# Attention scores in fp32 on four row tiles instead of bf16 parts, in a kernel of two expert layers and one windowed attention

## What is computed

```python
x = x + 0.5 * ffn(layernorm(x))       # top-1 router, 16 experts, capacity 320 in token order, gelu
x = x + attn(layernorm(x))
x = x + 0.5 * ffn(layernorm(x))

def attn(x):                          # 8 query heads, 4 key heads, head size 16
    q, k, v = rope(x @ Wq), rope(x @ Wk), x @ Wv      # each key head serves 2 query heads
    scores = q @ k.T / 4
    scores += head_scales * (q[..., :3] @ head_dirs) * (k[..., :3] @ head_dirs)
    allowed = (j <= i) & ((j < 4) | (j >= i - 127))   # window of 128 and 4 sinks
    return softmax(where(allowed, scores, -inf)) @ v @ Wo
```

## Time and profile before

| | us |
|---|---|
| median of 3 runs | 583.79 (583.53 to 583.94) |
| span of the profiled execution | 586.0 |
| PE busy | 462.1 (79%) |
| DVE busy | 349.6 (60%) |
| ACT busy | 319.4 (55%) |
| POOL busy | 225.0 (38%) |

### The profile page before, as it was taken

How to read it: one execution, slowest core, us unless ns; L and a number is a source line. 1 busy time by engine, 2 the same in 40 slices (tenths; PEclk the granted TensorE clock), 3 DMA queues, 4 the chain that set the end, 5 groups by cost and what they waited for, 6 DMA issues and landing times.

```text
span 586.0 us, 11013 instructions
## 1 busy us (share of the span) xinstructions
PE 462.1 (79%) x3044; PEld 308.3 (53%) x3044; DVE 349.6 (60%) x1848; ACT 319.4 (55%) x651; POOL 225.0 (38%) x270
## 2 busy tenths in 40 slices
PE   4554399999545689889798888978999867999991
PEld 2443167667323455556565555656565434776670
DVE  4764133333227887889989898898866452234320
ACT  4343043444314468697877868777785632443430
POOL 3677203544734232230623435152111340153555
PEclk9999999999967679999999999999897857999996
DMA  9831135564425100000000000000000012555430
GB/s 278 257 134 52 57 96 166 153 178 133 128 81 204 54 2 1 4 17 2 20 14 25 11 13 23 10 25 15 24 11 29 17 42 74 155 154 161 136 121 30
DMA packets 44697, 45.54 MB, mean 78 GB/s; under 512 B 4919, under 2 KB 34128, under 8 KB 44616
## 3 DMA queue, kind: packets, MB, share of 16 engines
q1 hardware_dynamic: 40040, 36.74, 20.6%
q0 software_dynamic: 4608, 8.22, 4.3%
HBM read 29.22 MB, written 19.17 MB: 83 GB/s over the span
## 4 chain that ended last, share of the span: by engine, by line
PE 47%; DVE 25%; issue 11%; ACT 6%; POOL 5%; DMA 3%; SPq 1%; POOLq 0%; DVEq 0%; ACTq 0%
PE sc L607 11%; DVE junk L1287 7%; PE b L617 7%; PE b L596 4%; PE b L775 3%; PE sc L741 3%; POOL slots L1484 2%; PE sc L744 2%; PE sc L715 2%; PE b L562 2%; PE b L631 2%; POOL out L1504 2%; ACT qT L1033 2%; PE sc L543 2%; ACT qT L1013 1%
## 5 line engine op out<-in xcount | busy, mean ns | idle before, releaser
L1287 DVE CUSTOM_DVE_ANT_0 junk<-sc,cht 128x256 bf16<-128x256 f32 (+1 forms) x256 | 82.4, 383 | 11.7 <-PE sc L715 11.0
L1484 POOL DMA_INDIRECT slots<-pay,slot_i x64 | 64.3, 1005 | 40.1 <-issue 19.0
L952 ACT ACTIVATE hT<-sc 128x320 f32<-128x320 f32 x128 | 56.0, 437 | 42.3 <-PE sc L607 29.7
L607 PE MATMUL sc<-enT,w1s 128*128 128x320 f32 x256 | 74.9, 437 | 0.5 <-issue 0.4
L617 PE MATMUL b<-hT,w2s 128*128 128x320 f32 x256 | 73.8, 432 | 0.0
L1504 POOL DMA_INDIRECT x<-yrow,ytok x40 | 38.9, 971 | 57.5 <-DVE yrow L1261 46.5
L1504 POOL DMA_INDIRECT out<-yrow,ytok x40 | 38.9, 972 | 57.4 <-DVE yrow L1261 46.4
L741 PE MATMUL sc<-cht 128*128 128x512 bf16 (+1 forms) x128 | 47.1, 374 | 16.9 <-DVE mx L1287 16.5
L607 PEld LDWEIGHTS sc<-enT,w1s 128*128 128x128 f32 x256 | 47.6, 190 | 21.4 <-issue 3.3
L617 PEld LDWEIGHTS b<-hT,w2s 128*128 128x128 f32 x256 | 47.4, 190 | 17.7
L1025 ACT ACTIVATE probs<-sc 128x1024 f32<-128x1024 f32 x48 | 49.1, 1025 | 11.3 <-PE sc L744 11.1
(11 more groups left out here) (165 smaller groups left out, 993.8 us busy)
## 6 DMA issues: line engine op xcount, KB each, us to landing
w1s<-in_L_ffn_w SPq DMA_DIRECT2D x32, 256.0 KB
w2s<-in_L_ffn_w SPq DMA_DIRECT2D x32, 256.0 KB
slots<-fresh SPq DMA_DIRECT2D x16, 330.0 KB, 4.4
rows<-slots SPq DMA_DIRECT2D x16, 330.0 KB
xall<-in_L_attn_x SPq DMA_DIRECT2D x8, 256.0 KB
xall<-x SPq DMA_DIRECT2D x8, 256.0 KB, 2.7
out<-xall SPq DMA_DIRECT2D x8, 256.0 KB
slots<-pay,slot_i POOLq DMA_INDIRECT x64
```

Source lines behind the costliest of these rows:

```text
L607: mm(hid[f], w1s[a][:, P * f:P * (f + 1)], enT[:, :, HALF * a:HALF * (a + 1)], start=True, stop=True).then_inc(e_hid, 1)
L952: nc.scalar.activation(hT[a][:, f, :], hid[f], ACT.Gelu_apprx_tanh).then_inc(e_gelu, 1)
L1287: ins = v.tensor_tensor_reduce(junk[:, H // 2 * h + i, lo:], sc[h][:, i // G, 2 * P * (i % G) + lo:2 * P * (i % G + 1)], tab16["window"][: ...
L1484: gp.indirect_dma_start(out=slots_d[phase], out_offset=bass.IndirectOffsetOnAxis(ap=slot_i[s][:, t:t + 1], axis=0), in_=pay[s][:, t, :], i ...
```

## The change

q, k and the maximum stay fp32. The rotation writes q and k into `qk` (three buffers), where each head has a place of 32 columns: 16 of the head, the 17th for the negated maximum (constant 1 for k), the rest zero. Wq's columns, the head directions and scales are put in an order in which the four heads that lie side by side belong to the four key heads. One fp32 turn of 128 columns then gives four heads in four groups of 32 rows, and a product over 16 rows uses one row tile of the array.

- `turn_qk` turns q and k (three fp32 turns), `qk_copy` copies them at once. `least` writes the negated maximum into the 17th column of `qk`, and `turn_qn` turns q once more with it (two turns, `qn_copy`).
- `both_scores` replaces `scores` and `turned_scores`. It is called twice a step: with the fresh scores of key heads 0 and 1 of tile c in `sc[0]` beside the turned ones of key heads 2 and 3 of tile k - 1 in `sc[1]`, and later the fresh ones of 2 and 3 in `sc[1]` beside the turned ones of 0 and 1 of tile k in `sc[0]`. The two masks come first, then fresh and turned products in turn.
- The second tile's sinks lie in the tile before it, so they are let through by a mask of their own (`window1`, `turned_window1`). Only tiles 2 and 3 have the separate sinks, from two products over all 128 rows (`sink_keys`, `sink_scores`).
- `part`, `part_rest`, `stack`, the split of the maximum and `max_copy` go. `values` also waits for the output of the tile before, `turn_sums` writes into the upper half of `b5`, `sink_values` stands behind the turns, `bend` and `means` on DVE stand between the two halves of `maxima`. POOL clears `qk` at the start.

```diff
-            def turned_scores(n, t, h, more):
-
-                pe.wait_ge(nm_copied, n + 1)
-                if more:
-
-                    pe.wait_ge(s_maxed, (n + 1) * 2 + h + 1)
...
+            def score(t, j, g):
                 lo = 0 if t else P
+                rows_j = slice(RG * j, RG * j + HD)
+                bank = sc[j // 2][:, j % 2, :].rearrange("p (g k) -> p g k", g=G)
+                return mm(bank[:, g, lo:2 * P], qkT[rows_j, t, P * g:P * (g + 1)],
+                          qkT[rows_j, t - 1:t + 1, G * P:] if t else qkT[rows_j, t, G * P:],
+                          start=(g == 0), stop=(g == G - 1), skip_group_check=True)
+
+            def turned_score(t, j, kb):
+                rows_j = slice(RG * j, RG * j + HD + 1)
+                bank = sc[j // 2][:, j % 2, :].rearrange("p (b g q) -> p b g q", b=2, g=G)
+                return mm(bank[:, kb], qkT[rows_j, t - 1 + kb, G * P:], qnT[t % 2][rows_j], start=False, stop=(kb == 1), skip_group_check=True)
+
+            def both_scores(c, tc, k, t, h):
+
+                fresh_half, old_half = has(c, TILES), has(k, TILES)
+                if old_half:
+                    pe.wait_ge(qn_copied, k + 1)
+                    masks(k, t, 1 - h, c * 2 + h if fresh_half else c * 2)
+                if fresh_half:
+                    pe.wait_ge(qk_copied, c + 1)
+                    if c == 1:
+                        pe.wait_ge(s_maxed, 1 + h)
+                    wait(pe, st_exp, c * 2 - 3 + h)
+                for i in range(2):
                     for jj in range(2):
+                        if fresh_half:
+                            last_s = score(tc, 2 * h + jj, i)
+                            if i and jj:
+                                last_s.then_inc(s_ready, 1)
+                    for jj in range(2):
+                        if old_half and (i or t):
+                            last_t = turned_score(t, 2 * (1 - h) + jj, i)
+                            if i and jj:
+                                last_t.then_inc(st_ready, 1)
...
+                    both_scores(c, tc, k - 1, te, 0)
+                    if has(k, TILES):
+                        turn_qn(k, t, b)
+                    if has(f, TILES):
+                        turn_sums(f)
+                    if has(d, TILES):
+                        turn_qk(d, td, bd, b, t + 2)
                     if t == 1 and has(b, B):
                         sink_values(b)
-                    if has(c, TILES):
-                        scores(c, tc)
-                    if has(e, TILES) and te:
-                        turn_sinks(te, be, b)
-                    if has(c, TILES) and tc:
+                    if has(c, TILES) and tc >= SINK_FROM:
                         sink_scores(tc, b)
...
+                    both_scores(c, tc, k, t, 1)
+                    if has(k, TILES) and t >= SINK_FROM:
+                        turn_sinks(t, b)
                     if has(e, TILES):
                         values(e, te)
```

365 lines of the change are left out of this document (151 added, 214 removed).

## The result

The changed kernel takes **618.9 us** (median of four executions, 610.6 to 656.4) against 583.7 for the kernel before, a ratio of 1.060 of the medians. By the two executions at the higher clock alone (610.6 and 614.7 us) it is 1.054, 95% interval 1.043 to 1.065. The forecast was 572. The direction was wrong; the time lies inside the range. The four executions differ far more than those of the kernel before, and in step with TensorE's granted clock: 610.6 us at a mean clock of 0.889, 614.7 at 0.890, 623.1 at 0.861 (the profiled one, span 621.2), 656.4 at 0.803. That scatter is itself a finding, and the experiments come back to it.

The account below looks back on a forecast made before the run. No engine is full: PE and DVE hand work round a loop, and PE's order with two waits for the maxima sets the new step. Batches -7.5, start -5.5, end +1: -12.0 us, 583.8 to 572; range 561 to 622.

Parts of the forecast that it names:

- rivals 1 (0.43 a round): Row-tiled scores: weights load one row tile at a time, 0.43 us a round, +54 us, 626 us; chance 17%.
- 2 (0.28): Row-tiled scores: three tiles run at a time, not four, 0.28 us a round, +15 us, 587 us; chance 12%.
- 4 (no overlap): Row-tiled scores: records do not overlap, 0.21 us each, 6.8 us a tile; chance 5%.
- the first round: Each group of row-tiled scores: three rounds in 0.66 us, the first priced at 0.22 us like the others.
- t=0: First tile's step of a batch: 8.45 us, against 9.25 in the kernel before.
- t=3: Fourth tile's step of a batch: 7.95 us, against 8.50 in the kernel before.
- First turned mask: Start of attention: first turned scores near 194.4, where they started at 199.69; -5.5 us.
- second: ... projection 7.65: Second tile's step: `vsink` ahead of the maxima, projection done at 7.65, step 8.5 us against 8.10 before.
- third: ... 7.85: Third tile's step: DVE reaches `base` of the routing at 7.85, projection waits for it; step 8.1 us against 8.53.
- the 0.3 allowed for gaps: Batch of four steps: 0.3 us added for semaphore gaps to the sum of 33.0, giving 33.3 us.
- the 2.95 of the second step: Second tile's step: maxima start at 2.95 us and not 1.62, since `vsink` stands ahead of them on DVE.
- rival 3, the clock: TensorE's clock in the loop: one stretch of 7 us a batch at 2.3 us, +17 us; chance 9%.

Follow-up runs that it names:

- h_afill: The changed kernel plus idle TensorE products over all rows where it waits in the loop, waits unchanged: 590.0 us, 1.035 of the kernel before.
- g_after: The changed kernel unedited, measured again as the level for the first group of experiments: 633.5 us, 1.11 of the kernel before.
- j_after: The changed kernel unedited, measured once more on one chip beside the last runs: 624.7 us, 1.075 of the kernel before.
- j_afill: The changed kernel plus idle TensorE work alone, on the same chip as j_after: 602.1 us, 1.036 of the kernel before.
- g_cvs: The changed kernel with `sink_values` back at the head of step t=1 and the sink scores copied out of b7: 602.9 us, 1.055 of the kernel before.
- g_vs: The changed kernel with only `sink_values` moved back to the head of step t=1: 605.5 us (583.0 to 611.5).
- g_copy: The changed kernel with only the sink scores copied out of b7 into SBUF, which sets the bank free: 635.7 us (625.6 to 640.3).
- h_fill: g_cvs plus idle TensorE products over all rows in the loop's waits: 576.9 us, 1.013 of the kernel before.
- h_best: h_fill with turned scores over 32 rows and idle products outside the loop too: 565.2 us, 0.992 of the kernel before; on another chip 576.1 us, 0.986.
- b_gaps: The kernel before plus idle products ahead of the two expert stages and of attention: 570.6 us, ratio 1.000.

## Why the prediction was wrong

**Right: the unknown price that it was built on.** Rounds of four row tiles are 0.22 us apart, so rivals 1 (0.43 a round), 2 (0.28) and 4 (no overlap) are out; the 0.28 by the Trainium skill's 3.07x (TensorE: Matmul & The Clock Gate, Measured speedup vs the span model) did not come. The mode change costs 0.09 or 0.10: the masks of h_afill and of the changed kernel stream until 0.43 after their start and the first row-tiled record stands 0.52 to 0.53 after it (321.20 to 321.73). Only the first round was under-priced: 0.32 to the second, not 0.22, so 0.1 a group, 0.2 a step. That is what steps t=0 (8.66 against 8.45) and t=3 (8.20 against 7.95) are off by.

**Right: start, unloading, order.** First turned mask at 192.96, forecast near 194.4 (-6.7 us, forecast -5.5). DVE and ACT fell as forecast, and the maxima release the second group. The forecast's 4.55 us from the first to the second group in t=1 is what the traces have (334.20 to 338.75).

**Wrong: the terms "second: ... projection 7.65" and "third: ... 7.85".** The prediction listed on DVE the least and the difference of the sinks in t=2, and took PE to wait only for `base`. It never asked who holds b7. The sink scores of the next tile sit in b7 until `psd`; the routing's ranks (L563) and the projection write the same bank. In t=1 the projection so stands 8.53 us after the step's start (334.20 to 342.73) and not 7.65. Step t=1 is 9.69 and not 8.5, t=2 8.67 and not 8.1. All four: 35.2 us at the upper clock against 33.3, **1.9 us a batch, 14 us in 7.5 batches**: enough by itself to turn the -12 into about +2.

Of these 14 us the bank is worth 7: the copy out of b7 brings 0.94 us a batch, all of it in t=1. In t=2 the wait for `psd` costs nothing in the end, since with the copy the step is still 8.67: `base` comes 8.2 us after the step's start with and without it, and not at 7.85. The rest is the under-priced first rounds, 0.2 in each of four steps, and this later `base`, less the 0.3 allowed for gaps. That both edits together bring the batch to 33.28, the forecast's figure, is chance: moving `sink_values` takes away 1.0 us that the forecast had in its sum (the 2.95 of the second step).

**Wrong by its size and its chance: rival 3, the clock.** The mechanism was named, with one stretch of 7 us a batch at 2.3 us, +17, and 9%. The price of one stretch was good: 6.8 us at half clock made the batch shown 37.3 us and not 35.2, 2.1 more. But there is more of it than one stretch a batch, some 30 us in a row from 240 us on. In the profiled execution 172 us are at half clock against 85: 87 x 0.37 = **32 us**, and the sum that gave 572 had nothing for it. 572 + 14 + 32 = 618 falls 5 short of that execution; that it meets the 618.9 of the median is partly luck, since the four executions have 135 to 258 us at half clock. The reason given against it, "the loop's PE load stays near 85%", was true of the trace and no argument: PE was busy in 85% in the kernel before as well, its scores over 96 and 108 rows. The change turned the scores into products over 16 and 17 rows, and it made waits longer. The runs speak for both. Idle work over 128 rows in the waits brings 43 us back (g_after to h_afill, two chips) and 23 on one chip (j_after to j_afill); 32 rows in place of 17 bring 19 us on top of g_cvs (two chips) and 13 in the median on one chip; idle work over 16 rows brings nothing. Of the waits it is shown for the one before `vsink` (g_vs), and not for the one for `psd` (g_copy). How the 32 us divide between rows and waits stays open.

Why the clock falls in one execution and not in the next of the same instructions (583 or 612 us for g_vs) stays open too. Not tried was letting the fresh scores use 32 rows too: their 17th row carries the maximum of an earlier tile.

## What to carry to other kernels

When a change moves the last use of a PSUM bank, list every engine that waits for that bank before you price the step: here one reader at the end of VectorE's step held up the projection and the routing. And see what waits next: of the two waits for `psd` only one gave time back, since `base` stood right behind the other. And when a change swaps wide products for narrow ones, give a fall of TensorE's clock a price and a good chance: the busy share of the page did not show it here (86% before, 88% after, from 210 to 410 us, at clocks of 0.99 and 0.85). Idle products over all rows in the waits are a quick test of what the clock costs (602 against 625 us on one chip). What a shorter wait brings can be lost again to the clock (g_copy), so look at the granted clock before you judge an edit by its time.

## What the runs showed of the hardware that was not expected

- In these runs the granted clock depends on the rows in use beside the time in use: PE busy in 197.95 of 200 us with narrow idle work at 0.83, in 193.21 with wide at 0.98; and rows of zeros count (0.897 to 0.908 against 0.817 to 0.866; on one chip a median of 0.888 against 0.864).
- Products to different row tiles pass each other: those issued later start 0.03 us after the first, and the order in the program changed no step by more than 0.02 us.
- Row tiles of fp32 with weights of 128 columns and 256 columns streamed: 0.32 us for the first round, 0.22 for the later ones, four side by side (332.28 to 333.04).
- One us at half clock costs the changed kernel 0.37 us between executions of it, and gave back 0.21 on the mean from h_fill to h_best, most of it outside the loop. In the kernel before the 14 us at half clock that b_gaps took away brought nothing (570.6 against 570.0).
